# Another order for the operations of the first three attention units on TensorE, ScalarE, VectorE and GpSimd

## The reference

```python
x = x + tanh(g_xattn) * attention(layernorm(x), ctx)
x = x + tanh(g_ffn) * experts(layernorm(x))      # top 2 of 8 experts

def attention(h, cond):                          # G = 8 groups, 2 heads each, D = 128
    ln = _ln(h, ln_w, ln_b)
    q  = _ln(fp8_linear(ln, wq));   k = _ln(fp8_linear(ln, wk));   v = fp8_linear(ln, wv)
    core = softmax(q k^T / sqrt(D)) v
    qx = _ln(fp8_linear(ln, wqx));  kx, vx = cond @ w_kv_x.T;      kx = _ln(kx)
    xout = softmax(qx kx^T / sqrt(D)) vx
    return fp8_linear(concatenate([core, xout]), wproj)
# fp8_linear: divide by a scale for each input, clip to +-448, round to the fp8 grid, multiply
```

## Time and profile before

| what | us |
|---|---|
| median of 3 runs | 685.33 |
| profiled execution | 686.1 |
| its span, first to last instruction | 684.3 |
| PE busy | 641.3 (94%) |
| DVE busy | 599.4 (88%) |
| ACT busy | 550.0 (80%) |
| POOL busy | 466.5 (68%) |

### The profile page before, as it was taken

The page is one execution under the profiler, slowest core; times in us unless marked ns, Lnnn a source line. Parts: engine busy times, 40 slices in busy tenths (PEclk is TensorE's granted clock), DMA queues, the critical chain, the costliest instruction groups (busy, mean ns, idle before and its releaser), DMA issues. The chain is left out here.

```text
span 684.3 us, 14974 instructions
## 1 busy us (share of the span) xinstructions
PE 641.3 (94%) x4573; PEld 588.8 (86%) x4574; DVE 599.4 (88%) x1386; ACT 550.0 (80%) x1927; POOL 466.5 (68%) x646
## 2 busy tenths in 40 slices
PE   1789999999999999999999999999998599999994
PEld 0788999999999999999999999999887588888883
DVE  7998899999999999998999999887799887777771
ACT  5898889899988998998899899988886256666660
POOL 4677786688767778777776886788665525565642
PEclk9999999999999999999999999999999589999998
DMA  7203010100020102002010110100089512333232
GB/s 228 62 2 93 2 32 1 40 25 32 2 62 1 32 2 63 32 1 64 1 32 2 55 43 2 61 3 1 1 300 399 172 39 47 47 54 54 46 46 24
DMA packets 35510, 37.73 MB, mean 55 GB/s; under 512 B 2704, under 2 KB 30352, under 8 KB 35440
## 3 DMA queue, kind: packets, MB, share of 16 engines
q1 hardware_dynamic: 31024, 30.84, 13.5%
q0 software_dynamic: 4416, 6.03, 5.5%
HBM read 31.62 MB, written 5.24 MB: 54 GB/s over the span
## 5 line engine op out<-in xcount | busy, mean ns | idle before, releaser
L1518 POOL TENSOR_SCALAR shared<-shared,rsum 128x256 f32<-128x256 f32 x256 | 143.8, 573 | 52.5 <-DVE rsum L1034 47.6
L717 ACT ACTIVATE shared<-s,nmax 128x256 f32<-128x256 f32 x256 | 122.3, 498 | 23.2 <-DVE nmax L1029 23.0
L1512 POOL TENSOR_TENSOR rstd<-rstd,half 128x7 f32<-128x7 f32 (+1 forms) x64 | 87.8, 1371 | 5.3
L1029 DVE TENSOR_REDUCE nmax<-s 128x2 f32<-128x512 f32 x128 | 86.6, 678 | 1.4 <-PE s L380 1.1
L1039 DVE TENSOR_TENSOR pt_lo<-t,pt_hi 128x512 fp32r<-128x512 f32 x124 | 84.1, 679 | 2.3 <-ACT pt_hi L725 1.3
L725 ACT CAST pt_hi<-t 128x512 fp32r<-128x512 f32 x124 | 73.9, 596 | 10.6 <-PE t L395 7.4
L733 ACT ACTIVATE shared<-route_bank,head_w 128x512 f32<-128x512 f32 (+1 forms) x124 | 81.7, 690 | 0.4 <-PE route_bank L409 0.4
L1024 DVE TENSOR_TENSOR qk_lo<-shared,qk_hi 128x512 fp32r<-128x512 f32 x96 | 77.9, 811 | 2.1 <-POOL qk_hi L1529 1.0
L380 PE MATMUL s<-qk_hi 128*128 128x256 f32 x256 | 77.3, 302 | 2.0 <-DVE qk_lo L1024 1.2
L336 PE MATMUL pj_a<-w_ring,xq 128*128 128x256 f32 x488 | 72.2, 291 | 6.3 <-POOL xq L1594 6.3
L395 PE MATMUL t<-ident,shared 128*128 128x128 f32 x496 | 75.0, 274 | 3.0 <-POOL shared L1518 1.7
(11 more groups left out here) (281 smaller groups left out, 1949.1 us busy)
## 6 DMA issues: line engine op xcount, KB each, us to landing
expert_w<-in_w SPq DMA_DIRECT2D x24, 512.0 KB, 9.3
spare<-in_wT SPq DMA_DIRECT2D x19, 256.0 KB, 3.0
wp_raw<-in_wpT SPq DMA_DIRECT2D x16, 256.0 KB, 2.9
spare<-in_wkvT SPq DMA_DIRECT2D x16, 128.0 KB, 3.3
spare<-in_wT SPq DMA_DIRECT2D x9, 128.0 KB, 3.2
spare<-in_x SPq DMA_DIRECT2D x1, 1024.0 KB, 5.9
x_hat<-acc SPq DMA_DIRECT2D x1, 1024.0 KB, 4.6
out<-spare SPq DMA_DIRECT2D x1, 1024.0 KB, 6.9
```

Source lines behind the costliest of these rows:

```text
L717: e = act.activation(probs[:, st, h * S:(h + 1) * S], s_bank[st][:, h * S:(h + 1) * S], ACT.Exp, bias=nmax[:, st, h:h + 1], accum_out=psum ...
L1029: dve.tensor_reduce(nmax[:, st, :], s_bank[st][:].rearrange("p (h t) -> p h t", h=2), AX, ALU.max, negate=True).then_inc(max_done, 1)
L1512: pool.tensor_tensor(rstd[:, st, c], rstd[:, st, c], half[:, c], ALU.pow).then_inc(rstd_ready, 1)
L1518: m = pool.tensor_scalar(probs[:, st, c], probs[:, st, c], rsum[:, st, h:h + 1], 1.0, ALU.mult, ALU.mult)
```

## The change

Nothing is added and nothing is removed; instructions change places within their own engine. On PE `project_kv(1, 0, 1, 1)` goes ahead of the wait for normq_done 3 and the five identity products of `stay_awake` (ten records in the trace). On ACT `affine_in(9)`, the v0 copy, `affine_in(13)`, `square(1)`, `row_scale(2)`, `weights_hi(1, 1, 0/2/3)`, `affine_in(19)`, `affine_in(21)`, `copy_v0(0)` and `probs_hi(0, 0, 1)` move. On DVE the order of the constants and of `row_stats(1)` changes, and the places of `clip_in`, `round_in`, `ctx_rest(0)`, `row_max`, `row_sum`, `normalise_kv(1, 1, 0)`, `rest_v0(0)` and of the two single products for the gate. On POOL `widen_in(0)`, `row_shift(2)`, `widen_in(10)` and `scale_probs(0, 0, 1)` move.

```diff
@@ -489,10 +489,10 @@
             pe.wait_ge(xq_y, 20)
             pe.wait_ge(v0_ready, 1)
             project_v0(pt_bank, 0)
+            pe.wait_ge(aff_done, 3)
+            project_kv(1, 0, 1, 1, pj_b, 1)
             pe.wait_ge(normq_done, 3)
             stay_awake(o_bank, 5)
-            pe.wait_ge(aff_done, 3)
-            project_kv(1, 0, 1, 1, pj_b, 1)
             scores(0, 0, 1, 0)
             scores(0, 0, 1, 1)
             stay_awake(o_bank, 4)
@@ -807,27 +807,27 @@
             affine_in(7)
             row_scale(1)
             affine_in(8)
+            affine_in(9)
             weights_hi(0, 0, 2)
             weights_hi(0, 0, 3)
             weights_hi(0, 0, 0)
+            act.wait_ge(v0_scaled, 1)
+            act.copy(v0_w[:, 0], v0_raw).then_inc(v0_high, 1)
             split_ctx(0)
             weights_hi(0, 0, 1)
-            affine_in(9)
             affine_in(10)
-            split_ctx(1)
             affine_in(11)
             affine_in(12)
-            act.wait_ge(v0_scaled, 1)
-            act.copy(v0_w[:, 0], v0_raw).then_inc(v0_high, 1)
             affine_in(13)
+            split_ctx(1)
             affine_in(14)
             affine_in(15)
             square(0)
+            square(1)
+            weights_hi(1, 1, 0)
+            split_ctx(2)
+            square(2)
             row_scale(2)
-            square(1)
-            split_ctx(2)
-            weights_hi(1, 1, 0)
-            square(2)
             weights_hi(1, 1, 1)
             affine(0, 0, s_bank[0])
             act.wait_ge(v0_ready, 1)
@@ -835,27 +835,27 @@
             affine_in(16)
             affine_in(17)
             affine_in(18)
-            weights_hi(1, 1, 2)
             affine_in(19)
-
             act.wait_ge(ctx_split, 3)
             affine(0, 2, pj_b)
+
+            weights_hi(1, 1, 2)
             affine_in(20)
+            affine_in(21)
             exps(0, 0, 0)
-            affine_in(21)
             exps(0, 0, 1)
             affine_in(22)
+            copy_v0(0, pt_bank)
             affine_in(23)
-            copy_v0(0, pt_bank)
             square(3)
             probs_hi(0, 0, 0)
             exps(0, 1, 0)
-            weights_hi(1, 1, 3)
             act.wait_ge(stats_ready, 4)
             act.wait_ge(rstd_ready, 3)
             square_q(2, 0, o_bank)
+            probs_hi(0, 0, 1)
             exps(0, 1, 1)
-            probs_hi(0, 0, 1)
+            weights_hi(1, 1, 3)
             square_kv(2, 2, 0, acc_bank)
             affine(1, 0)
             act.wait_ge(stats_ready, 5)
@@ -1180,44 +1180,44 @@
             dve.wait_ge(cols_loaded, 32)
             dve.reciprocal(inv_in[:], col[:, C_INS:C_INS + 8]).then_inc(inverted, 1)
             dve.reciprocal(inv_smooth[:], col[:, C_SMOOTH:C_SMOOTH + 32]).then_inc(inverted, 1)
+            dve.wait_ge(inverted, 2)
+            dve.tensor_scalar(inv_smooth[:], inv_smooth[:], GRID, None, ALU.mult)
+            row_normalise(0)
             dve.wait_ge(cols_loaded, 32)
             for i in range(4):
                 dve.tensor_scalar(head_w[:, 2 * i:2 * i + 2], col[:, C_HLN + 2 * i:C_HLN + 2 * i + 2],
                                   float(D) ** -0.5 if i < 2 else 1.0, None, ALU.mult)
-            row_normalise(0)
-            dve.wait_ge(inverted, 2)
-            dve.tensor_scalar(inv_smooth[:], inv_smooth[:], GRID, None, ALU.mult)
             for i in range(4):
                 v = inv_in[:, i * KT:(i + 1) * KT]
                 dve.scalar_tensor_tensor(in_scale[:, i * KT:(i + 1) * KT], v, GRID, col[:, C_LNW:C_LNW + KT], ALU.mult, ALU.mult)
                 m = dve.scalar_tensor_tensor(in_shift[:, i * KT:(i + 1) * KT], v, GRID, col[:, C_LNB:C_LNB + KT],
                                              ALU.mult, ALU.mult)
             m.then_inc(consts_ready, 1)
-            row_stats(1)
             dve.wait_ge(ones_set, 2)
             for i, blks in enumerate(((0, 1), (2, 3), (4,), (7,))):
                 for n in blks:
                     m = dve.tensor_tensor(w_scale[:, :, n], col[:, C_INS + i * KT:C_INS + (i + 1) * KT],
                                           col[:, C_SCAL + i:C_SCAL + i + 1].broadcast_to([P, KT]), ALU.mult)
             m.then_inc(w_scales_ready, 1)
+            row_stats(1)
             clip_in(0)
             round_in(0)
             sum_weights(0, 1)
             clip_in(1)
             sum_weights(0, 0)
             round_in(1)
-            clip_in(2)
             dve.wait_ge(w_scales_ready, 1)
             centre_weights(0, 0, (0, 1, 2, 3) + later_blocks(0))
+            clip_in(2)
             dve.wait_ge(v0_loaded, 16)
             dve.tensor_tensor(v0_raw, v0_raw, w_scale[:, :, 7:8].broadcast_to([P, KT, D]), ALU.mult).then_inc(v0_scaled, 1)
-            round_in(2)
             weights_lo(0, 0, 2)
             weights_lo(0, 0, 3)
+            clip_in(3)
+            weights_lo(0, 0, 0)
             ctx_rest(0)
-            weights_lo(0, 0, 0)
             weights_lo(0, 0, 1)
-            clip_in(3)
+            round_in(2)
             round_in(3)
             row_stats(2)
             ctx_rest(1)
@@ -1228,16 +1228,16 @@
             clip_in(7)
             round_in(5)
             round_in(6)
+            round_in(7)
             dve.wait_ge(v0_high, 1)
             dve.tensor_tensor(v0_w[:, 1], v0_raw, v0_w[:, 0].bitcast(F32), ALU.subtract).then_inc(v0_ready, 1)
-            round_in(7)
-            dve.wait_ge(gated, 1)
-            dve.tensor_tensor(gate[:, 1:2], col[:, C_SCAL + S_PROJ:C_SCAL + S_PROJ + 1],
-                              col[:, C_SCAL + S_PIN:C_SCAL + S_PIN + 1], ALU.mult).then_inc(gated, 1)
             sum_weights(1, 0)
             centre_weights(1, 0, (0, 1, 2, 3))
             centre_weights(1, 0, later_blocks(1))
             normalise_q(0, 0, 0, early_banks[0][0])
+            dve.wait_ge(gated, 1)
+            dve.tensor_tensor(gate[:, 1:2], col[:, C_SCAL + S_PROJ:C_SCAL + S_PROJ + 1],
+                              col[:, C_SCAL + S_PIN:C_SCAL + S_PIN + 1], ALU.mult).then_inc(gated, 1)
             normalise_kv(0, 0, 0, early_banks[0][1])
             sum_weights(1, 1)
             centre_weights(1, 1, (0, 1, 2, 3))
@@ -1253,29 +1253,31 @@
             round_in(9)
 
             clip_in(10)
-            row_max(0, 0, 0)
             clip_in(11)
             round_in(10)
+            row_max(0, 0, 0)
+            round_in(11)
             normalise_q(1, 1, 0, early_banks[2][0])
-            round_in(11)
+            clip_in(12)
             row_max(0, 0, 1)
+            round_in(12)
+            split_heads(0, 0, 2)
             row_sum(0, 0, 0)
-            clip_in(12)
-            split_heads(0, 0, 2)
-            round_in(12)
+            clip_in(13)
             normalise_kv(1, 1, 0, early_banks[2][1])
-            clip_in(13)
+            row_sum(0, 0, 1)
             round_in(13)
             clip_in(14)
-            row_sum(0, 0, 1)
+            dve.wait_ge(gated, 2)
+            dve.tensor_tensor(attn_gate[:], gate[:, 0:1], gate[:, 1:2], ALU.mult).then_inc(gated, 1)
+            rest_v0(0, pt_bank)
+            round_in(14)
             clip_in(15)
-            round_in(14)
-            rest_v0(0, pt_bank)
             round_in(15)
             row_max(0, 1, 0)
-            row_max(0, 1, 1)
             probs_lo(0, 0, 0)
             row_sum(0, 1, 0)
+            row_max(0, 1, 1)
             dve.wait_ge(xq_ready, 16)
             normalise_q(1, 1, 1)
             weights_lo(1, 1, 0)
@@ -1283,13 +1285,11 @@
             weights_lo(1, 1, 2)
             weights_lo(1, 1, 3)
             normalise_kv(1, 1, 1)
+            row_sum(0, 1, 1)
             probs_lo(0, 0, 1)
             normalise_q(2, 2, 0, o_bank)
             split_heads(1, 1, 0)
-            row_sum(0, 1, 1)
             normalise_kv(2, 2, 0, acc_bank)
-            dve.wait_ge(gated, 2)
-            dve.tensor_tensor(attn_gate[:], gate[:, 0:1], gate[:, 1:2], ALU.mult).then_inc(gated, 1)
             split_heads(1, 1, 1)
             rest_v0(1, s_bank[1])
 
@@ -1597,8 +1597,8 @@
             pool.wait_ge(ones_set, 1)
             row_power(0)
             row_power(1)
+            widen_in(0)
             row_shift(1)
-            widen_in(0)
             centre_first()
             widen_in(1)
             widen_in(2)
@@ -1606,11 +1606,11 @@
             wp_hi(0, 0, 0)
             row_power(2)
             widen_in(4)
-            row_shift(2)
             widen_in(5)
             widen_in(6)
             widen_in(7)
             power(0, 0)
+            row_shift(2)
             wp_lo(0, 0, 0)
             pool.wait_ge(normkv_done, 1)
             power(0, 1)
@@ -1620,14 +1620,14 @@
             power(1, 0)
             widen_in(8)
             widen_in(9)
+            widen_in(10)
             heads_hi(0, 0, 2)
-            widen_in(10)
 
             widen_in(11)
             scale_probs(0, 0, 0)
             widen_in(12)
+            scale_probs(0, 0, 1)
             widen_in(13)
-            scale_probs(0, 0, 1)
```

## The result

The changed kernel takes 687.57 us (median of 20 runs, 685.54 to 690.85) against 685.36 (20 runs, 684.95 to 686.71) for the kernel before in the same session. The forecast was 685.5 with a range of 684.1 to 687.0 and a chance of 0.17 for slower. The loss is 2.2 us by the medians and 1.9 by the ratio (1.2 to 2.5), and the times also lie wider apart, 5.3 us against 1.8.

What follows compares the result with a forecast made beforehand. PE was taken to bound the loop, no one engine the prologue. Parts 1 and 2 gave +0.2 at the scores, part 3 passed it on as +0.2, part 4 added 0: 685.33 + 0.2, or 685.5 us, range 684.1 to 687.0.

Steps and rivals of the forecast that it cites:

- Part 1: 0 to 20 us, up to PE's first projection: start at 20.1 instead of 20.04, +0.06 us, bounds 19.9 and 20.5.
- Part 2: 20 to 36.6 us, to the first scores: scores at 36.75 instead of 36.56, +0.2 us, from -0.1 to +0.7.
- Part 3: 36.6 to 46.65 us, to the sixteenth xq: first row_sum at 42.0, POOL idle before it; +0.2 us, bounds -0.7 and +0.8.
- Part 4: 46.65 to 63 us, into the loop: power(2, 0) begins 0.5 us later, nearly all absorbed by later waits; adds 0.
- The first part of the prediction: PE alone paces the loop, so a microsecond in the prologue is worth at most one microsecond of the total.
- Rival (b): Slower: once the first row_sum ends after 42.1 us, each microsecond of it adds one; 687.0 us, chance 0.13.
- Rival (c): Slower: PE waits some 1.4 us before the first scores and its clock falls; +2.0 us, 687.3 us, chance 0.04.
- the bound of 1.37 us: On the whole time: the threshold between change and no change, 0.2%.

Runs made afterwards that it cites:

- a_again: The changed kernel run once more with no edit: 688.32 us, ratio 1.0039.
- a_awake: The changed kernel with identity products added on PE, 6 before the heads of unit 0 and 7 before the sixteenth xq: 687.66 us, ratio 1.0023.
- b_warm: The kernel before with sixteen identity products in PE's idle time ahead of the first projection: 685.45 us, ratio 0.9992.

## Why the prediction was wrong

**Part 1, to the first projection: right.** 20.15, where the sum said 20.1. The wider claim, that both widenings stand together in front of PE, is what POOL's row shows (one group of two, begun at 18.90).

**Part 2, to the scores: the right number from the wrong working.** The first `affine` came at 32.98 (33.2 forecast), the scores at 36.81 (36.75). But DVE, which was to wait 0.5 us for the heads, did not wait. POOL's and DVE's rows after:

```profile
33.91 0.71 POOL L1529 TENSOR_SCALAR qk_hi<-shared 128x512 fp32r<-128x512 f32 x1 [1.79 <-ACT shared L733]
```

```profile
35.01 0.68 DVE L1024 TENSOR_TENSOR qk_lo<-shared,qk_hi 128x512 fp32r<-128x512 f32 x1
```

The heads were ready at 34.62, and DVE came to them 0.4 us later. Two things were missed. First, the gate product: the prediction has no term for its new place, and it took 1.08 us instead of 0.145, beside a POOL product of 1.29 us (27.44 to 28.73; the gate product ended at 28.75). It ate what `normalise_q` had won (it began at 27.06 instead of 27.75). The prediction weighed such a meeting for two instructions of full length and did not ask about the short one. The Trainium skill ("SBUF — State Buffer", section "Who interferes with whom") calls the ports that the two engines share an exclusive lock, so that the one that comes second waits for the other's whole instruction, however short it is itself; the rows agree. Second, the sum took PE's end of the second half's products, 26.3, from the one profile. That moment is not a number but a spread: PE's full pace came 3.3 to 6.1 us behind q. `row_scale(2)`, which the change moves away, was the cover for exactly this; I priced its removal at the 0.25 us of idle that this one trace would give. In the first profile after, with the earliest pace of all, it cost ACT 0.04 (the first `affine` 12.83 us behind q instead of 12.79), in a_again 0.42, in a_awake 1.23. The upper bound of +0.7 was passed in three profiles (17.28, 17.28 and 17.42 against 16.52) and their mean with the others is +0.5: what I held for an end of the range is an ordinary value.

**Part 3, to the sixteenth xq: the failed step of the sum.** The order of events was right: row_sum late, POOL idle before it, then dense, PE waiting for `widen_in(15)`. Two terms were mis-sized. The row_sum was put at 42.0 and came at 42.55: ten clips and roundings were counted with one or two of them stretched beside POOL, and three were (37.52, 38.26 and 40.54, each 0.33 to 0.45 us longer than the 0.28 of one alone). The steps as listed, with the prediction's own pitch of 0.2 us for a clip or rounding, come to 4.8 to 5.2 us and not to 5.4; measured are 5.88 from the first clip at 36.67. And the hand-overs were left out: POOL's first scaling began 0.25 us behind the start of the row_sum, as it does before, and PE 0.06 behind POOL's last. The rest, 4.89 us, lay inside the 4.5 to 5.1. So from 42.0 + 4.85 = 46.85 the sum goes to 42.55 + 0.25 + 4.89 + 0.06 = 47.75. I took +0.2 "near the lower end" against my own trend, with the argument that moved clips meet POOL less; they met it more. The term was put at +0.2 and measured +0.85, over its bound of +0.8 by 0.05.

**Part 4, into the loop: right.** The late `weights_hi(1, 1, 3)` on ACT held `power(2, 0)` back and was absorbed. From u2 to the accumulate of unit 1 it is 48.24 us before and 48.25 after, and the distance of 1.1 us, once there, is neither paid off nor added to. The first part of the prediction holds too: a microsecond at the entry of the loop is a microsecond of the total.

**Rival (b), the late row_sum, was the case that came true in kind,** with its decision point (row_sum after 42.1) and its line: each microsecond behind it is one of the total. It was held for a heap of bounds at 0.13; the ordinary values of its terms were enough to pass that point.

**Rival (c), PE's clock, was right in kind and wrong in place: the sum has no term for it.** It looked at the wait before the scores, put at 1.4 us; that wait was 0.82 and left the clock alone. The wait that grew was the next one, 0.66 to 1.79 us. The prediction moved u2 by 0.2 and did not ask what PE does meanwhile. PE's work ahead of it ends at 45.96 (45.99 before), so each microsecond by which `widen_in(15)` slips is a microsecond of idle. Its size is 1.27 to 1.30 and not 2.0. Its chance, 0.04, was set by one row that showed no fall. For such a wait the runs give one execution in two. The Trainium skill, "TensorE: Matmul & The Clock Gate", section "HAM oscillation — how this bites in real kernels", that was cited for it, describes the fall as one that recurs with each wait; here the same kernel shows it in one execution and not in another.

**The whole.** The fixed terms alone, 1.1 us, would have stayed within the bound of 1.37 us and within the range; the two terms that vary carried the median past both. A single trace contains neither, so the range, built from the terms of one execution, was too narrow at its upper end.

## What to carry to other kernels

An instruction whose place looks free in one trace may be the cover for a moment that varies from execution to execution: before it is moved, ask what ends behind it (here PE's slow start, 3.3 to 6.1 us), and price it at the late end. Where a chain ends at a wait of PE, follow what PE does during the delay as well as the delay itself, since a wait grown from 0.66 to 1.8 us can cost about its own growth again in granted clock. A product of one element per partition is not free either when it is put beside a long instruction of POOL: ask what it will stand next to. When two profiles are compared, compare those in which PE reached its pace at the same distance. And count hand-overs and stretched instructions at the rate that the rows next to them show, since two queues that share the work (row_sum and the roundings here) give little back when only one of them is mended.

## What the hardware showed that was not expected

- PE's granted clock fell behind a wait of only 1.5 to 1.8 us, at 48 to 52 us, in three profiles of six, to 0.57, 0.59 and 0.66, and cost 1.27 to 1.30 us each time. It fell in none of ten with a wait of 0.67 us or less. PE had been busy from the scores at 36.8 with waits of less than a microsecond.
- After the 6.4 us of idle at 20 us PE ran at little more than half pace (eight matmuls in 2.08 us instead of 1.21) for 3.3 to 6.1 us while its granted clock read 1.00. Identity products ahead of it took this away (1.22 us in b_warm) and moved nothing behind it in the kernel before.
- A DVE product of one element per partition took 1.08 us at one place, 0.56 at another and 0.145 at a third, by what POOL was running. The 1.08 us put DVE's queue last on the way to the first scores.
- The profiled execution of the changed kernel was faster than that of before although its median is 2.2 us slower. Most of what hid it lies 500 us behind the change: the passage at 530 to 554 us, granted clock 0.72 against 0.57.
